# Second cross attention, selection: exponentials already normalised on ScalarE, one head of four selected on GpSimd

## The chip, the cores and the metric

The kernel runs on one core of a Trainium2 chip. The metric is the device time of one launch in microseconds; less is better. Engines are named as in the profile: PE is TensorE, DVE is VectorE, ACT is ScalarE, POOL is GpSimd and SP is SyncE.

## The reference

The program is two layers of a small perceiver (cross attention, self attention, feed forward, twice) on `x` of 4 batches x 256 rows x 256. The change is in the cross attention of the second layer, which has 4 heads and reads a context of 4096 rows of 192 per batch:

```python
scores = einsum('bthd,bghd->bhtg', Q, K) / sqrt(32)        # 4096 per row and head
scores = where(vision_mask, scores, -inf)
topv, topi = top_k(scores, 32)
probs = softmax(topv)
attn = zeros_like(scores).at[..., topi].set(probs)
attn_mean = attn.mean(axis=1)                               # over the 4 heads
c_t = einsum('btg,bgd->btd', attn_mean, context @ Wv)
```

So each row keeps its 32 largest scores per head, weights them by a softmax over these 32, and the four heads are averaged.

## The kernel before

The stage is `stage_x1a`. A step p (0 to 15) is a batch, one of its two blocks of 128 rows, and two heads h; four steps make a batch, and two steps (p even, then p odd) make one block's mean over four heads. The score tile `SC[p % 2]` is 128 x 2 x 4096 in float32 and there are two of it; the first lies in S0, so the trace calls the two S and SC. Three tiles `PM` hold exponentials, two tiles `ACC` the means. Every engine runs the same loop over iterations n = 0 to 19, in its own fixed order:

- TensorE in iteration n: `flag(n-2)`; for n >= 4 the transposes (`turn(m, g)`, eight per mean tile m, four in an even n and four in the following odd n) and the products with the context (`product(m, g)`, eight matmul records each); the scores of step n in eight chunks of 512 columns (`scores(n, ch)`), into two PSUM slots. In odd iterations the four products come ahead of the scores, in even ones between them. In n % 4 = 3 and n % 4 = 0 it also projects the next batch's keys (`keys`, four chunks each).
- ScalarE: copies transposes (`turned`), score chunks (`copy(n, ch)`) and key chunks out of PSUM, copies a product's sum (`done`), and computes `weigh(n-1, h)`, an exponential of 128 x 4096 in one instruction, after chunks 3 and 6 (L1661). `copy(n, 0)` waits until VectorE has selected step n-2, since they share a score tile.
- VectorE: for step n-1 and each head, 32 MAX8 over 128 columns each (`candidates`, L1731) and then `top`, a chain of small instructions that finds the 32nd largest value T8 and whether the shortcut was valid (L1736 to L1750); for step n-2, `check` (a flag from TensorE, a branch that is normally skipped) and two `select`s (L1776: exponential times (score >= T8), 4096 wide, with the row sum as a second output). The selects stand after 32 of head 0's candidates in even n, after 16 in odd n.
- GpSimd for every selected head: the reciprocal of the sum by a power (L1847), a scaling by it and by 1/4 (L1852 or L1855), and an addition into `ACC` (L1857). The last step is added by VectorE (`add`, L1794).
- SyncE loads the context tiles `CN` for the products; each load waits for an earlier product.

`turn(m, 0)` and `turn(m, 4)` wait for the finished sum of step 2m+1. In n % 4 = 1 VectorE also normalises the next query (XN, L1717), in n % 4 = 3 it makes a mask row (MR, L1724). In this text e(p, h) is the exponential of step p and head h.

The order of ScalarE around the change is written out by hand:

```python
if ch in (3, 6) and 0 <= n - 1 < NP:
    weigh(n - 1, ch // 6)
```

Of the kernel before, what the change touches and what calls it, by code (L numbers as in the profile page):

```python
# [123 lines left out]
def build(nc, dr, spec, out):  # L124
    ctx = ExitStack()
    with ctx:
# [1347 lines left out]
        def stage_x1a(c, x1a, S0, t_x1c):  # L1474
# [6 lines left out]
            ACC = [sbt(c, f"ACC{i}", [128, NK]) for i in range(2)]  # L1481
            CN = [sbt(c, f"CN{i}", [128, 4, 192]) for i in range(2)]
# [12 lines left out]
            ON1, NG1 = sbt(c, "ON1", [128, 1]), sbt(c, "NG1", [128, 1])  # L1495
# [7 lines left out]
            FLAG, NMAX, SUM, REC = range(4)  # L1503
# [3 lines left out]
            QV, MRV, GI = sig("x1_query"), sig("x1_mask_row"), sig("x1_pool_set")  # L1507
# [32 lines left out]
            def by_vector(p, h):  # L1540

                return p == NP - 1

            def summed(p, k):
                return V.at(("sum", p, 1, k)) if by_vector(p, 1) else G.at(("sum", p, 1))
# [99 lines left out]
            def scalar(e):  # L1645
# [41 lines left out]
                for n in range(NP + 4):  # L1687
                    nb_ = query(n)
                    m, gs = context(n)
                    if nb_ is not None:  # L1690
                        q_turned(nb_)
                    for g in gs[0:2 if n % 2 == 0 else 4]:
                        turned(m, g)
                    if nb_ is not None:
                        q_copy(nb_)
                    if m is not None and gs[3] == 7:
                        done(m)
                    for ch in range(8):
                        if n % 4 == 0 and rekeyed(n, ch):
                            keys["scalar"](e, bank, *rekeyed(n, ch))  # L1700
                        if n < NP:
                            copy(n, ch)
                        if n % 4 == 3 and rekeyed(n, ch):
                            keys["scalar"](e, bank, *rekeyed(n, ch))
                        if m is not None and n % 2 == 0 and ch in (3, 5):
                            turned(m, gs[2 + (ch - 3) // 2])
                        if ch in (3, 6) and 0 <= n - 1 < NP:
                            weigh(n - 1, ch // 6)

            def vector(e):  # L1710
# [41 lines left out]
                def check(p):  # L1752
# [6 lines left out]
                    e.wait_ge(*S.at(("e", p, 1)))  # L1759
# [3 lines left out]
                    with e.If_ne(reg["v"], 2 * 128 * 8):  # L1763
                        for h in range(2):
                            for r8 in range(4):
                                e.max(t8[:, h, 8 * r8:8 * r8 + 8], sc[:, h, :])
                                e.drain()
                                e.match_replace(sc[:, h, :], t8[:, h, 8 * r8:8 * r8 + 8], sc[:, h, :], SENT)
                                e.drain()
                            e.tensor_scalar(sc[:, h, :], sc[:, h, :], 0.9 * SENT, None, ALU.is_le)  # L1770
                            e.memset(t8[:, h, 31:32], 0.5)
                            e.drain()

                def select(p, h):
                    pm = PM[(2 * p + h) % 3]
                    e.scalar_tensor_tensor(pm[:, :], SC[p % 2][:, h, :], T8[p % 2][:, h, 31:32], pm[:, :], ALU.is_ge, ALU.mult,  # L1776
                                           accum_out=SM[p % 3][:, h, SUM:SUM + 1]).then_inc(*V.up(("sel", p, h)))

                def add():

                    p = NP - 1
                    sm, acc = SM[p % 3], ACC[1]
                    for h in range(2):
                        rc = sm[:, h, REC:REC + 1]
                        e.wait_ge(*V.at(("sel", p, h)))
                        e.tensor_scalar(rc, sm[:, h, SUM:SUM + 1], 4.0, None, ALU.mult).then_inc(*V.up())
                        e.wait_ge(*V.now())
                        e.reciprocal(rc, rc).then_inc(*V.up())
                    e.wait_ge(*G.at(("sum", p - 1, 1)))
                    for k in range(2):  # L1790
                        part = slice(k * NK // 2, (k + 1) * NK // 2)
                        for h in range(2):
                            e.wait_ge(*V.now())
                            e.scalar_tensor_tensor(acc[:, part], PM[(2 * p + h) % 3][:, part], sm[:, h, REC:REC + 1], acc[:, part], ALU.mult, ALU.add).then_inc(*V.up(("sum", p, h, k)))  # L1794
# [18 lines left out]
                for n in range(NP + 4):  # L1813
# [4 lines left out]
                    for h in range(2):  # L1818
                        for g in range(32):
# [12 lines left out]
            def gpsimd(e):  # L1832
                e.memset(NG1[:, :], -1.0).then_inc(*GI.up())
# [3 lines left out]
                for p in range(NP):  # L1837
                    b, k, hp = place(p)
                    for h in range(2):
                        if by_vector(p, h):  # L1840
                            continue
                        pm, sm, acc = PM[(2 * p + h) % 3][:, :], SM[p % 3], ACC[k]
                        rc = sm[:, h, REC:REC + 1]
                        e.wait_ge(*V.at(("sel", p, h)))
                        if p + h == 0:
                            e.wait_ge(*GI.now())
                        e.tensor_tensor(rc, sm[:, h, SUM:SUM + 1], NG1[:, :], ALU.pow).then_inc(*G.up())  # L1847
                        if hp + h == 0:
                            if b > 0:
                                e.wait_ge(*M.at(("t", 2 * (b - 1) + k, 7)))  # L1850
                            e.wait_ge(*G.now())
                            e.tensor_scalar(acc[:, :], pm, rc, 0.25, ALU.mult, ALU.mult).then_inc(*G.up(("sum", p, h)))  # L1852
                        else:
                            e.wait_ge(*G.now())
                            e.tensor_scalar(pm, pm, rc, 0.25, ALU.mult, ALU.mult).then_inc(*G.up())  # L1855
                            e.wait_ge(*G.now())
                            e.tensor_tensor(acc[:, :], acc[:, :], pm, ALU.add).then_inc(*G.up(("sum", p, h)))  # L1857

            def sync(e):
# [12 lines left out]
                def context_in(m, g):  # L1872
# [5 lines left out]
                    elif g < 5:  # L1878
                        e.wait_ge(*V.at(("sel", NP - 2, 1)))
# [8 lines left out]
                for n in range(NP + 4):  # L1888
# [16 lines left out]
                    if n == NP + 1:  # L1905
                        e.wait_ge(*V.at(("sel", NP - 2, 1)))
# [959 lines left out]
```

## Time and profile before

| | us |
|---|---|
| median of 3 runs | 2086.05 |
| lowest, highest run | 2084.93, 2088.73 |
| time of the profiled execution | 2084.4 |
| its span | 2082.6 |
| first and last instruction of the selection, L1731 to L1794 | 1151.9 to 1700.5 |

The profiled execution's time is 1.8 us more than its span. A row of the timeline gives the start, the duration and the instruction; `x32` behind it means that so many were merged, and the bracket gives the idle time ahead of it and what ended it.

### The profile page before, as it was taken

The numbers are of one execution on the slowest core, as the hardware profiler recorded it, in microseconds if no ns is written. First come the engines' busy times: TensorE is split into PE (matmuls) and PEld (weight loads), VectorE is DVE, ScalarE is ACT, GpSimd is POOL, SyncE is SP. The second block draws the span as 40 slices with busy tenths as digits, with TensorE's granted clock in tenths as the row PEclk, the third lists the DMA queues.
The fourth block names the chain that finished last, engine by engine and source line by source line (L and its number), as shares of the span: only waits on it lengthen the run. The fifth ranks groups of instructions, "written<-read, shape, count | busy, mean of one in ns | idle before, by whom it ended". The sixth has DMA issues, their size and how long they took to land.

```text
span 2082.6 us, 34689 instructions
## 1 busy us (share of the span) xinstructions
PE 1755.0 (84%) x13676; PEld 1114.9 (54%) x13676; DVE 1214.4 (58%) x2969; ACT 1025.3 (49%) x1391; POOL 753.6 (36%) x660
## 2 busy tenths in 40 slices
PE   6889999999999998888788868777777658987884
PEld 3445655565565555565577325344553455776663
DVE  5154241415333202636784698999999967547776
ACT  2578578667766991211311545546565521114542
POOL 6364334414533400000300076978779721110001
PEclk9999999999999998999788557788886779999987
DMA  7865649655664712000100003122231251000000
GB/s 153 168 114 125 136 110 139 136 117 123 131 129 102 112 61 80 2 1 2 54 1 6 9 16 86 52 85 76 69 93 37 74 189 68 0 1 1 1 6 16
DMA packets 80061, 150.01 MB, mean 72 GB/s; under 512 B 15464, under 2 KB 65448, under 8 KB 73480
## 3 DMA queue, kind: packets, MB, share of 16 engines
q1 hardware_dynamic: 64304, 101.80, 17.1%
q0 software_dynamic: 12336, 41.41, 12.9%
q10 hardware_dynamic: 3240, 4.35, 0.8%
q8 instruction: 118, 1.93, 0.4%
q14 instruction: 63, 0.52, 0.1%
HBM read 93.59 MB, written 2.62 MB: 46 GB/s over the span
## 4 chain that ended last, share of the span: by engine, by line
PE 62%; DVE 23%; POOL 4%; ACT 4%; issue 3%; DMA 2%; ACTq 0%; DVEq 0%; POOLq 0%; SPq 0%
PE R L112 37%; PE B L112 22%; DVE CA L1731 5%; DVE PM L1776 5%; PE B L178 2%; POOL ACC L1857 2%; DVE CA L1743 1%; DVE T L1745 1%; ACT PS L2415 1%; ACT PM L1661 1%; DMA CN<-in_ctxn 1%; DMA KST<-OV 1%; DVE MX L2571 1%; POOL PM L1855 1%; DVE A L1067 1%
## 5 line engine op out<-in xcount | busy, mean ns | idle before, releaser
L629 ACT ACTIVATE P<-R 128x1024 f32<-128x1024 f32 x512 | 500.8, 1028 | 128.0 <-PE R L112 113.7
L112 PE MATMUL R<-QS,KST 100*128 100x256 bf16 x2048 | 270.7, 275 | 13.0 <-issue 7.4
L112 PE MATMUL B<-P,VP 128*32 128x256 f32 x4096 | 277.4, 387 | 1.4 <-issue 1.1
L112 PEld LDWEIGHTS R<-QS,KST 100*128 100x128 bf16 x2048 | 182.0, 98 | 138.5 <-issue 64.6
L1857 POOL TENSOR_TENSOR ACC<-ACC,PM 128x4096 f32<-128x4096 f32 x22 | 195.1, 8869 | 1.8
L200 POOL TENSOR_TENSOR LNrs<-LNve,pk_const 128x2 f32<-128x2 f32 x36 | 25.3, 703 | 445.6 <-DVE LNve L196 445.3
L112 PE MATMUL R<-OV,QT 32*128 32x512 f32 x512 | 179.2, 786 | 0.0
L837 POOL DMA_DIRECT2D KST<-OV x300 | 144.5, 490 | 66.5 <-PE R L112 46.4
L112 PEld LDWEIGHTS B<-P,VP 128*32 128x32 f32 x4096 | 107.7, 109 | 102.5 <-issue 33.8
L1847 POOL TENSOR_TENSOR SM<-SM,NG 128x1 f32<-128x1 f32 x30 | 79.3, 2643 | 144.2 <-DVE PM L1776 144.2
L659 DVE CAST OV<-RT 128x512 bf16<-128x512 f32 x64 | 31.4, 490 | 168.4 <-ACT RT L116 99.7
L791 POOL CAST OV<-RT 128x512 bf16<-128x512 f32 x64 | 39.0, 610 | 207.1 <-DVE RT L661 207.1
L1731 DVE MAX8 CA<-S 128x8 f32<-128x128 f32 x512 | 101.8, 275 | 12.0 <-ACT S L116 11.6
L672 DVE COPY VP<-R 128x512 f32<-128x512 f32 x54 | 34.8, 686 | 126.8 <-PE R L112 126.8
L1731 DVE MAX8 CA<-SC 128x8 f32<-128x128 f32 x512 | 100.9, 276 | 6.6 <-ACT SC L116 6.0
L756 DVE RECIPROCAL RC<-B 128x256 f32<-128x256 f32 x16 | 28.0, 1751 | 119.1 <-PE B L112 119.1
L116 ACT ACTIVATE S<-R 128x1024 f32<-128x1024 f32 x64 | 64.1, 1024 | 61.4 <-DVE PM L1776 34.8
L112 PE MATMUL R<-CT,pk_x 128*128 128x512 f32 (+1 forms) x224 | 87.0, 636 | 6.8 <-ACT RT L116 6.8
L112 PE MATMUL R<-OV,ONB 1*128 1x512 bf16 x256 | 61.9, 480 | 35.9 <-ACT SC L116 22.0
L112 PEld LDWEIGHTS R<-OV,QT 32*128 32x128 f32 x512 | 64.0, 246 | 37.0 <-issue 29.5
L116 ACT ACTIVATE SC<-R 128x1024 f32<-128x1024 f32 x64 | 64.1, 1020 | 37.2 <-PE R L112 20.9
L1855 POOL TENSOR_SCALAR PM<-PM,SM 128x4096 f32<-128x4096 f32 x22 | 80.9, 3679 | 2.2
(346 smaller groups left out, 3374.1 us busy)
## 6 DMA issues: line engine op xcount, KB each, us to landing
KST<-OV POOLq DMA_DIRECT2D x276, 128.0 KB, 10.7
CT<-in_ctxP SPq DMA_DIRECT2D x40, 768.0 KB, 4.8
CN<-in_ctxn SPq DMA_DIRECT2D x60, 384.0 KB, 3.4
CT<-in_ctxT SPq DMA_DIRECT2D x64, 192.0 KB, 2.5
KST<-OV SPq DMA_DIRECT2D x84, 128.0 KB, 8.9
KST<-in_ctxP ACTq DMA_DIRECT2D x4, 768.0 KB, 8.0
pk_a<-in_pk_a SPq DMA_DIRECT2D x1, 3014.0 KB, 9.7
OV<-in_pk_x1b SPq DMA_DIRECT2D x1, 2944.5 KB, 9.9
```

Source lines behind the costliest of these rows:

```text
L112: return e.matmul(o, l, r, start=st, stop=sp, skip_group_check=True)
L116: return e.activation(o, i, ACT.Copy)
L178: return e.transpose(o, i, ident[0:n, 0:n])
L629: e.activation(P[(32 * p + k0) % 3][:, :], ring.at(("s", p, k0))[:, :], ACT.Exp).then_inc(*EX.up((p, k0)))
L672: e.tensor_copy(o, v).then_inc(*VC.up((b, 4 * ch + h + 2 * i)))
L791: e.tensor_copy(KS[1][:, cs], rt[:, :]).then_inc(*KG.up())
L837: e.dma_start(KST[buf][16 * s:16 * s + 16, hh, cols], KS[SLOT_K[s]][r0:r0 + 16, cols]).then_inc(*S[buf].up((b, g) if hh == hs[-1] and s == ...
L1731: e.max(CA[:, g * 8:g * 8 + 8], SC[p % 2][:, h, g * 128:g * 128 + 128]).then_inc(*V.up())
L1776: e.scalar_tensor_tensor(pm[:, :], SC[p % 2][:, h, :], T8[p % 2][:, h, 31:32], pm[:, :], ALU.is_ge, ALU.mult, accum_out=SM[p % 3][:, h, SU ...
L1847: e.tensor_tensor(rc, sm[:, h, SUM:SUM + 1], NG1[:, :], ALU.pow).then_inc(*G.up())
L1855: e.tensor_scalar(pm, pm, rc, 0.25, ALU.mult, ALU.mult).then_inc(*G.up())
L1857: e.tensor_tensor(acc[:, :], acc[:, :], pm, ALU.add).then_inc(*G.up(("sum", p, h)))
```

## The change

- `weigh(p, h)` on ScalarE becomes four activations: an exponential of the 32 kept values with their sum as a second output, `Ln` of four times that sum, `Identity` that makes the bias (minus maximum, minus logarithm), and the exponential of 128 x 4096 with this bias, which then comes out divided by four times the row sum. It waits for the end of `top` (`fl`) where it waited for its third instruction (`nm`).
- `weigh(n-1, 0)` stands after chunk 5 (before: 3), and `weigh(n-1, 1)` at the very start of iteration n+1, ahead of everything else of ScalarE (before: after chunk 6 of n).
- The weights of p even, h = 0 are written straight into `ACC`; the scaling and the power of GpSimd, and the sums of `select`, are gone.
- For p even, h = 1, VectorE no longer selects. GpSimd makes a mask in bfloat16 (`MK`, score >= T8), multiplies the exponential by it, and adds. `copy(n, 0)` then waits for that mask (n even) and for the exponentials of step n-2.
- The selects stand after 16 candidates of head 0 in every n. `check` no longer waits for the exponential; each `select` does.
- The branch that is normally skipped has a longer body. `add` becomes four plain additions. The scratch area of the descriptors of GpSimd's DMAs is set to 4096 bytes.

The diff, cut to its core (the rest follows from these lines):

```diff
+            MK = sbt(c, "MK", [128, NK], BF16)
+            TE = sbt(c, "TE", [128, 32])
+            def weights(p, h):
+                return (ACC[p // 2 % 2] if p % 2 + h == 0 else PM[2 * (p % 2) + h - 1])[:, :]
+            def by_gpsimd(p, h):
+                return p % 2 == 0 and h == 1
...
                 def weigh(p, h):
-                    i = 2 * p + h
-                    if i >= 3:
-                        e.wait_ge(*G.at(("sum", *divmod(i - 3, 2))))
-                    e.wait_ge(*V.at(("nm", p, h)))
-                    e.activation(PM[i % 3][:, :], SC[p % 2][:, h, :], ACT.Exp, bias=SM[p % 3][:, h, NMAX:NMAX + 1], scale=RS).then_inc(*S.up(("e", p, h)))
+                    sm = SM[p % 3][:, h, :]
+                    e.wait_ge(*V.at(("fl", p, h)))
+                    e.activation(TE[:, :], T8[p % 2][:, h, 0:32], ACT.Exp, bias=sm[:, NMAX:NMAX + 1], scale=RS, accum_out=sm[:, LSUM:LSUM + 1]).then_inc(*S.up())
+                    e.wait_ge(*S.now())
+                    e.activation(sm[:, LSUM:LSUM + 1], sm[:, LSUM:LSUM + 1], ACT.Ln, scale=4.0).then_inc(*S.up())
+                    e.wait_ge(*S.now())
+                    e.activation(sm[:, BIAS:BIAS + 1], sm[:, LSUM:LSUM + 1], ACT.Identity, bias=sm[:, NMAX:NMAX + 1], scale=-1.0).then_inc(*S.up())
+                    if p % 2 + h == 0 and p >= 4:
+                        e.wait_ge(*M.at(("t", (p - 4) // 2, 7)))
+                    if p % 2 + h > 0 and p >= 2:
+                        e.wait_ge(*G.at(("sum", p - 2, h)))
+                    e.wait_ge(*S.now())
+                    e.activation(weights(p, h), SC[p % 2][:, h, :], ACT.Exp, bias=sm[:, BIAS:BIAS + 1], scale=RS).then_inc(*S.up(("e", p, h)))
                 def copy(p, ch):
                     if ch == 0 and p >= 2:
-                        e.wait_ge(*V.at(("sel", p - 2, 1)))
+                        e.wait_ge(*(G.at(("mask", p - 2)) if by_gpsimd(p - 2, 1) else V.at(("sel", p - 2, 1))))
+                        e.wait_ge(*S.at(("e", p - 2, 1)))
...
+                    if 0 <= n - 2 < NP:
+                        weigh(n - 2, 1)
                     if nb_ is not None:
                         q_turned(nb_)
...
-                        if ch in (3, 6) and 0 <= n - 1 < NP:
-                            weigh(n - 1, ch // 6)
+                        if ch == 5 and 0 <= n - 1 < NP:
+                            weigh(n - 1, 0)
...
                 def select(p, h):
-                    pm = PM[(2 * p + h) % 3]
-                    e.scalar_tensor_tensor(pm[:, :], SC[p % 2][:, h, :], T8[p % 2][:, h, 31:32], pm[:, :], ALU.is_ge, ALU.mult,
-                                           accum_out=SM[p % 3][:, h, SUM:SUM + 1]).then_inc(*V.up(("sel", p, h)))
+                    e.wait_ge(*S.at(("e", p, h)))
+                    e.scalar_tensor_tensor(weights(p, h), SC[p % 2][:, h, :], T8[p % 2][:, h, 31:32], weights(p, h), ALU.is_ge, ALU.mult).then_inc(*V.up(("sel", p, h)))
...
-                            if h == 0 and g == (31 if n % 2 == 0 else 15) and 0 <= n - 2 < NP:
+                            if h == 0 and g == 15 and 0 <= n - 2 < NP:
                                 check(n - 2)
                                 select(n - 2, 0)
-                                select(n - 2, 1)
+                                if not by_gpsimd(n - 2, 1):
+                                    select(n - 2, 1)
...
+                for p in range(NP - 1):
+                    acc = weights(p - p % 2, 0)
                     for h in range(2):
+                        pm = weights(p, h)
+                        if p % 2 + h == 0:
                             continue
+                        e.wait_ge(*V.at(("sel", p, 0 if by_gpsimd(p, h) else h)))
+                        if by_gpsimd(p, h):
                             e.wait_ge(*G.now())
+                            e.tensor_scalar(MK[:, :], SC[p % 2][:, h, :], T8[p % 2][:, h, 31:32], None, ALU.is_ge).then_inc(*G.up(("mask", p)))
+                            e.wait_ge(*S.at(("e", p, h)))
                             e.wait_ge(*G.now())
+                            e.tensor_tensor(pm, pm, MK[:, :], ALU.mult).then_inc(*G.up(("product", p)))
+                        e.wait_ge(*G.now())
+                        e.tensor_tensor(acc, acc, pm, ALU.add).then_inc(*G.up(("sum", p, h)))
...
-    nc = _bacc.Bacc("TRN2", target_bir_lowering=False, num_devices=1)
+    nc = _bacc.Bacc("TRN2", target_bir_lowering=False, num_devices=1, dynamic_dma_scratch_size=4096)
```

## Rows read from the trace of the kernel before

**Rows 1.** Windows, sum of iterations n=6 to 9: us, then busy us.

```profile
sum 131.10, PE 99.10 PEld 62.59 DVE 125.35 ACT 75.46 POOL 103.37; mean PE 24.77 PEld 15.65 DVE 31.34 ACT 18.86 POOL 25.84
```

**Rows 2.** The chain that ended last, stretch 1322 to 1454.

```profile
by line: DVE CA L1731 37.8%; DVE PM L1776 28.1%; DVE CA L1743 8.5%; DVE T L1745 8.3%; DVE CA L1748 3.4%; issue 3.0%; DVE XN L1717 2.2%; DVE T L1737 2.1%; DVE MR L1724 1.9%; DVE SM L1750 1.6%; DVE SM L1736 1.3%; DVEq L1762 0.9%; DVE SM L1739
```

**Rows 3.** Groups of instructions, 1167 to 1721: busy us, mean ns, idle before.

```profile
L1857 POOL TENSOR_TENSOR ACC<-ACC,PM 128x4096 f32<-128x4096 f32 x22 | 195.1, 8869 | 1.8
...
L1731 DVE MAX8 CA<-SC 128x8 f32<-128x128 f32 x512 | 100.9, 276 | 6.6 <-ACT SC L116 6.0
...
L1855 POOL TENSOR_SCALAR PM<-PM,SM 128x4096 f32<-128x4096 f32 x22 | 80.9, 3679 | 2.2
...
L1776 DVE SCALAR_TENSOR_TENSOR PM<-SC,T,PM 128x4096 f32<-128x4096 f32 x16 | 72.1, 4541 | 9.2 <-ACT PM L1661 3.8 <-DVE FI L1757 3.6 <-ACT S L116 1.8
...
L116 ACT ACTIVATE SC<-R 128x1024 f32<-128x1024 f32 x64 | 64.1, 1020 | 37.2 <-PE R L112 20.9 <-DVE PM L1776 14.3 <-DVE CA L1731 1.7
L1661 ACT ACTIVATE PM<-SC,SM 128x4096 f32<-128x4096 f32 x16 | 59.3, 3707 | 9.7 <-DVE SM L1739 9.7
```

**Rows 4.** Timeline, GpSimd and VectorE, n=6: start us, us, instruction.

```profile
1322.10 8.83 POOL L1857 TENSOR_TENSOR ACC<-ACC,PM 128x4096 f32<-128x4096 f32 x1
...
1329.84 5.38 DVE L1776 SCALAR_TENSOR_TENSOR PM<-S,T,PM 128x4096 f32<-128x4096 f32 x1 [0.59 <-DVE FI L1757]
...
1335.15 4.47 DVE L1776 SCALAR_TENSOR_TENSOR PM<-S,T,PM 128x4096 f32<-128x4096 f32 x1
1335.31 4.73 POOL L1847 TENSOR_TENSOR SM<-SM,NG 128x1 f32<-128x1 f32 x1 [4.37 <-DVE PM L1776]
```

**Rows 5.** Timeline, VectorE: one top(), and the start of iteration n = 9.

```profile
1350.42 0.21 DVE L1736 TENSOR_REDUCE SM<-CA 128x1 f32<-128x32 f32 x1
...
1354.53 0.27 DVE L1750 TENSOR_SCALAR SM<-SM,T 128x1 f32<-128x1 f32 x1
...
1420.34 2.89 DVE L1717 TENSOR_SCALAR XN<-X,MV,RSD 128x256 f32<-128x256 f32 x2
```

**Rows 6.** Timeline, ScalarE: small activations and table loads.

```profile
1769.23 1.28 ACT L2087 ACT_TABLE_LOAD   x1
...
1878.60 0.20 ACT L2435 ACTIVATE EDA<-pk_qf 128x1 f32<-128x1 f32 x1 [19.94 <-PEq L183]
...
1878.93 1.28 ACT L2438 ACT_TABLE_LOAD   x1
1880.22 0.20 ACT L2438 ACTIVATE EDA<-EDA 128x1 f32<-128x1 f32 x1
...
1888.16 0.19 ACT L2415 ACTIVATION_READ_ACCUMULATOR PS<-R,MX 128x1 f32 x1
```

**Rows 7.** Timeline, TensorE: iterations n = 7, 8 and 9 at the full clock.

```profile
1368.79 0.39 PE L112 MATMUL R<-OV,ONB 1*128 1x512 bf16 x2
...
1379.41 1.99 PE L112 MATMUL B<-CT,pk_x1a 96*128 96x256 f32 x8
...
1404.11 1.57 PE L112 MATMUL R<-CN,AT 128*128 128x192 f32 x8
...
1415.00 1.02 PE L112 MATMUL R<-OV,QT 32*128 32x512 f32 x4
...
1428.70 1.57 PE L112 MATMUL R<-CN,AT 128*128 128x192 f32 x8 [0.74 <-ACT AT L116]
...
1435.66 1.54 PE L112 MATMUL R<-CN,AT 128*128 128x192 f32 x8 [0.32 <-DMA CN<-in_ctxn]
```

**Rows 8.** Timeline, TensorE at iteration n = 10, after a wait for GpSimd.

```profile
1462.37 1.94 PE L178 MATMUL B<-pk_const,ACC 128*128 128x128 f32 x8 [7.82 <-POOL ACC L1857]
...
1468.62 2.93 PE L112 MATMUL R<-CN,AT 128*128 128x192 f32 x8
```

**Rows 9.** Windows, n=10 after that wait: busy us, granted clock, DMA.

```profile
1462.40:1472.40 10.00, 10.00 (x34) 6.35 (x36) 9.90 (x10) 2.63 (x4) 5.63 (x2) 0.50 0.01 2
```

More of the change, by code:

```diff
@@ L1494, in stage_x1a @@
             SM = [sbt(c, f"SM{i}", [128, 2, 4]) for i in range(3)]
[L1495 removed]
+            TE = sbt(c, "TE", [128, 32])
+            ON1 = sbt(c, "ON1", [128, 1])
             ONB = sbt(c, "ONB", [128, 128], BF16)
@@ L1538, in query @@
                 return n // 4 + 1 if n % 4 == 1 and n // 4 + 1 < NB else None
-            def by_vector(p, h):
-                return p == NP - 1
+            def weights(p, h):
+                return (ACC[p // 2 % 2] if p % 2 + h == 0 else PM[2 * (p % 2) + h - 1])[:, :]
+            def by_gpsimd(p, h):
+                return p % 2 == 0 and h == 1
             def summed(p, k):
-                return V.at(("sum", p, 1, k)) if by_vector(p, 1) else G.at(("sum", p, 1))
+                return V.at(("sum", p, 1, k)) if p == NP - 1 else G.at(("sum", p, 1))
             def tensor(e):
@@ L1772, in check @@
                             e.drain()
+                            total = t8[:, h, 33:34]
+                            e.scalar_tensor_tensor(weights(p, h), sc[:, h, :], 0.5, weights(p, h), ALU.is_ge, ALU.mult, accum_out=total)
+                            e.drain()
+                            e.tensor_scalar(total, total, 4.0, None, ALU.mult)
+                            e.drain()
+                            e.reciprocal(total, total)
+                            e.drain()
+                            e.tensor_scalar(weights(p, h), weights(p, h), total, None, ALU.mult)
+                            e.drain()
                 def select(p, h):
-                    pm = PM[(2 * p + h) % 3]
-                    e.scalar_tensor_tensor(pm[:, :], SC[p % 2][:, h, :], T8[p % 2][:, h, 31:32], pm[:, :], ALU.is_ge, ALU.mult,
-                                           accum_out=SM[p % 3][:, h, SUM:SUM + 1]).then_inc(*V.up(("sel", p, h)))
+                    e.wait_ge(*S.at(("e", p, h)))
+                    e.scalar_tensor_tensor(weights(p, h), SC[p % 2][:, h, :], T8[p % 2][:, h, 31:32], weights(p, h), ALU.is_ge, ALU.mult).then_inc(*V.up(("sel", p, h)))
                 def add():
                     p = NP - 1
[L1782 to L1788, printed above, removed]
+                    acc = weights(p - 1, 0)
+                    e.wait_ge(*V.now())
                     e.wait_ge(*G.at(("sum", p - 1, 1)))
@@ L1792, in add @@
                         for h in range(2):
+                            e.tensor_tensor(acc[:, part], acc[:, part], weights(p, h)[:, part], ALU.add).then_inc(*V.up(("sum", p, h, k)))
                             e.wait_ge(*V.now())
-                            e.scalar_tensor_tensor(acc[:, part], PM[(2 * p + h) % 3][:, part], sm[:, h, REC:REC + 1], acc[:, part], ALU.mult, ALU.add).then_inc(*V.up(("sum", p, h, k)))
                 def stats(n, a0, a1):
@@ L1878, in context_in @@
                     elif g < 5:
-                        e.wait_ge(*V.at(("sel", NP - 2, 1)))
+                        e.wait_ge(*G.at(("mask", NP - 2)))
                     else:
@@ L1905, in sync @@
                     if n == NP + 1:
-                        e.wait_ge(*V.at(("sel", NP - 2, 1)))
+                        e.wait_ge(*G.at(("mask", NP - 2)))
                         for g in (2, 3, 4):
```

24 lines of the change are left out of this document (3 added, 21 removed).

## The prediction

> **What bounds the kernel now.** I read three views of the stage. The windows first: four iterations (n = 6 to 9, two steps p even and two odd) take 131.1 us, and VectorE is busy for 125.35 of them, GpSimd for 103.4, TensorE for 99.1, ScalarE for 75.5 [rows 1]. Then the chain that ended last over the same stretch: nearly all of it is VectorE's candidates and selects [rows 2]. So a microsecond taken from VectorE there is worth one, until another engine's own order becomes longer. The groups give the prices [rows 3]: 32 MAX8 take 6.3 us (their starts are 0.197 apart, 100.9 us busy over 512), a select 4.48, an addition on GpSimd 8.87, a one-input pass there 3.68, a full exponential 3.70, a copied score chunk 1.02. One `top` takes 4.4 us (from 1350.42 to 1354.80 [rows 5]).
>
> Third, the timeline shows what two engines do to each other. A select that met a running addition took 5.38 us instead of 4.48, and ended its wait where the addition ended; GpSimd's power beside a select took 4.73 us, until the select was over [rows 4]; XN took 2.89 us [rows 5]. So an addition or product of GpSimd and a select of VectorE exclude each other, whichever starts first keeps the other out for its whole length.
>
> **The change, engine by engine.** VectorE loses one select in four: 2 x 4.48 = 9.0 us per four iterations, some 0.5 us of read sums (6 selects without one) and the 0.9 us of that blocked select. If nothing else ended later, four iterations would take 131.1 - 10.4 = 120.7 us. The last additions stay at four halves of select's length. The 16 checks and their skipped branch stay, with a longer body that I take at nothing.
>
> GpSimd loses powers and scalings and gains a mask and a product. Per two steps, before: 103.4 / 2 = 51.7 us. After: three additions and a product at 8.87 and a mask at 3.68 (a one-input pass of that width; the bounds are 3.68 and 8.87, and I take the one-input row), 39.2 us [rows 1, 3]. It is not the bound.
>
> ScalarE gains in each of 32 `weigh`s: an exponential of 32 columns with its sum (0.20 for a tiny activation, and 0.19 to read the sum; I take 0.40), Ln 0.20, Identity with its bias from memory 0.30 (bounds 0.20 and twice that), and table loads. A load takes 1.28 us, and the activation behind it starts at once, 0.01 us later [rows 6]. The trace shows no Ln. The bounds are no load (all functions in one table) and two (to Ln's table and back). The nearest row is Tanh followed by Exp, two functions with a load between them, so I take two: 2.58 us. The sum is 3.48, a `weigh` takes 3.48 + 3.70 = 7.15 us net of the usual overlap. That is 8 x 3.45 = 28 us more ScalarE per four iterations, 103 of 131 busy. By busy time it fits. By order it does not, since ScalarE waits for TensorE inside the same iteration.
>
> The Trainium skill, "ScalarE: Activation LUTs", section "What ACT_TABLE_LOAD costs", puts a switch at 2.66 us with its drain; the rows show 1.28 and nothing behind it. By the page eight `weigh`s would cost 22 us more than in my sum; by the rows they don't.
>
> **Four iterations stepped through.** TensorE's runs between two things that ScalarE must do come from [rows 7]: from the first product of an even n to score chunk 5, keys in between, 11.9 us (1404.11 to 1416.02), 8.1 without the two key projections of 1.9; the four products of an odd n 8.5 us (1428.70 to 1437.20); six score chunks and three key projections 12.6 us (1368.79 to 1381.40), 6.6 without keys. During the old order ScalarE did an exponential amid these runs, so TensorE could get ahead; in the new one only chunks 6 and 7 are left behind each `weigh`. I start with n = 8 at 0, ScalarE 8.0 us late, and step on until the lateness repeats.
>
> n = 8: e(6,0) ends at 5.4, select(6,0) at 9.9, the mask at 13.6. Then half the candidates, `top`, the other head: VectorE reaches n = 9 at 28.1. ScalarE: e(6,1) at 15.15; transposes, keys and copies with TensorE to 29.2; e(7,0) at 36.4; the rest to 39.0. GpSimd multiplies from 15.15 and adds until 32.9.
>
> n = 9: e(7,1) ends at 46.1. XN waits for GpSimd until 32.9, and the flag for score chunk 7, which needs the key chunk that ScalarE copied at 37.0; so select(7,0) ends at 45.2. GpSimd has been waiting for it and starts its addition, 8.9 us. select(7,1) could start at 46.1, and starts at 54.1. It ends at 58.6, and VectorE reaches n = 10 at 76.8. Before, the second select followed the first at once and the addition came after. ScalarE: products, copies from 58.6, e(8,0) at 73.3, free at 75.3.
>
> n = 10: e(8,1) at 84.0, mask at 89.0, copies from there, e(9,0) at 105.0, free at 107.0. VectorE reaches n = 11 at 103.5, GpSimd's addition ends at 106.8.
>
> n = 11: MR waits for that addition, select(9,0) ends at 115.5. e(9,1) ends at 114.2, 1.3 us ahead of that, so select(9,1) follows at once, to 119.9; VectorE reaches n = 12 at 138.2. ScalarE: products to 123.3, scores and keys to 136, e(10,0) at 143.6, free at 146.2, again 8.0 late.
>
> So four iterations take 138.2 instead of 131.1 us, +7.1. The work of steps 1 to 15 has fourteen iterations, 3.5 times that: **+25 us**. What follows VectorE's last iteration (the last transposes, context loads and products) hangs on the last flag and additions, which keep their distance from it, and is as long as before. The profiled execution took 2084.4 us and should come to 2109; the median of the runs, 1.7 us above it, to 2111.
>
> **The rivals.** (a) *No table loads in the loop*, chance 0.12. Exp, Ln and Identity stay in one table. For it: Tanh at 1878.60 ran on the table loaded for Gelu at 1769.23. Against it: the load between Tanh and Exp [rows 6]. `weigh` then takes 4.6 us, ScalarE is back at VectorE's boundaries, select(7,1) is ready before select(7,0) ends, and VectorE's 120.7 us bound the loop: -10.4 x 3.5 = -36, 2050 us. The Trainium skill, "ScalarE: Activation LUTs", section "Table sets: the hidden batching unit", says that Exp and Ln share one set and cost one load; by that rule this rival would be the result.
>
> (b) *The loads fit*, two per `weigh` but VectorE still bounding, chance 0.08. It needs ScalarE some 3 us earlier per iteration, since otherwise e(7,1) misses the end of select(7,0). Then part of (a): -10, 2076.
>
> (c) *No change that can be told*, chance 0.10. A change under 0.2% (4.2 us) can't be told from none here. If e(7,1) came 1 us earlier, the addition would not get ahead of select(7,1), and the loop would be the longer of ScalarE's own: 8 x 7.15 and 74.5 of the runs, copies and transposes = 131.7, +2, 2088.
>
> (d) *The forecast*, chance 0.50, its own range 2096 to 2122.
>
> (e) *TensorE drops to its lower level*, chance 0.18. After 7.8 us of waiting in n = 10 its granted clock was 0.50 over ten us, the lower level, 1.2 GHz [rows 9], and eight product records took 2.93 us [rows 8] instead of 1.57 at 2.4 GHz [rows 7]. In the new order it stands still around each `weigh`, 5 us and more. If the first product, transposes and scores of each iteration run at that level, ScalarE slips by 3 to 4 us in each, and e(9,1) misses select(9,0) too, since its margin is 1.3 us. That is another 7 us per four iterations: +50, 2136, at worst 2150.
>
> (f) *The smaller scratch area stalls GpSimd's DMAs* in the first layer, chance 0.02. Its bursts there are short, and I give it +10.
>
> **How the numbers follow.** Slower are (d), (e), (f): 0.70. Same is (c): 0.10. Faster are (a) and (b): 0.20. The predicted time is that of (d), 2111. The range takes in (e) but for its worst, and goes down to (b) and part of what lies between it and (a): 2070 to 2142; left out are (a), 0.12, and some 0.06 above.
>
> **What would show it.** Two rows ACT_TABLE_LOAD per `weigh`, 64 in all, at 1.28. In n = 9 and its like, a select that starts some 8 us after the first ended, with "POOL" holding it back; in n = 11 none. VectorE's busy time in the stage down by some 35 us, and its idle time up by more. ScalarE busy about 100 of 138 us. Four iterations of 138 us. A prediction of slower is wrong if the loads are few, or if `weigh` takes under 6 us.

## The result, and the profile after

The changed kernel takes 2162.47 us (median of 4, 2150.79 to 2165.89) against 2087.39 for the kernel before (median of 4): the ratio is 1.0342, 95% interval 1.0291 to 1.0394. It is slower, as forecast, but by 75 us and not by 25. The profiled execution took 2165.89 us, its span is 2164.1. The page's first part:

```profile
PE 1804.4 (83%) x13676; PEld 1145.5 (53%) x13676; DVE 1207.6 (56%) x2925; ACT 1136.2 (53%) x1583; POOL 726.5 (34%) x615
```

I measure the selection from its first MAX8 over 128 columns to its last one. Before, that is one window (us, then busy us of PE, PEld, DVE, ACT, POOL, then TensorE's granted clock, DMA share, GB/s):

```profile
1151.90:1674.90 523.00, 389.39 (x1660) 226.20 (x1656) 481.02 (x1571) 284.21 (x247) 377.32 (x82) 0.73 0.22 65
```

The same window after, and three times four iterations within it:

```profile
1158.40:1751.10 592.70, 433.35 (x1660) 255.65 (x1656) 469.18 (x1533) 388.27 (x433) 342.02 (x37) 0.67 0.18 53
...
1221.30:1375.60 154.30, 115.11 (x398) 65.47 (x395) 124.95 (x391) 99.41 (x110) 94.48 (x11) 0.61 0.16 47
1375.60:1527.70 152.10, 111.47 (x474) 69.93 (x474) 124.83 (x391) 102.54 (x116) 94.54 (x11) 0.74 0.22 63
1527.70:1680.50 152.80, 117.84 (x466) 73.66 (x465) 117.29 (x387) 101.65 (x114) 94.44 (x11) 0.71 0.22 63
```

So 69.7 of the 81.5 us between the two spans lie in the selection; 6.5 lie ahead of it and 5.3 behind. Four iterations take 153.1 us (forecast 138.2, before 131.1 [rows 1]), and in them VectorE is busy for 122.4. It no longer bounds them. TensorE does the same instructions in 44 us more of busy time, at a granted clock of 0.67 and not 0.73. The groups that answer to [rows 3] and [rows 6] (busy us, mean ns, idle before):

```profile
L1871 POOL TENSOR_TENSOR ACC<-ACC,PM 128x4096 f32<-128x4096 f32 x22 | 207.3, 9423 | 90.9 <-DVE PM L1802 89.9
...
L1802 DVE SCALAR_TENSOR_TENSOR PM<-SC,T,PM 128x4096 f32<-128x4096 f32 x16 | 98.1, 6153 | 30.3 <-ACT PM L1675 26.0 <-DVE FI L1774 2.7 <-ACT SM L1669 0.9
L1866 POOL TENSOR_SCALAR MK<-S,T 128x4096 bf16<-128x4096 f32 x8 | 84.9, 10611 | 162.3 <-DVE ACC L1802 162.3
...
L1869 POOL TENSOR_TENSOR PM<-PM,MK 128x4096 f32<-128x4096 f32 x8 | 63.7, 7961 | 1.2
...
L1667 ACT ACT_TABLE_LOAD x32 | 41.1, 1283 | 0.6
L1675 ACT ACT_TABLE_LOAD x32 | 41.1, 1283 | 2.1
```

The mask costs 10.61 us, three times the forecast's 3.68. The 64 table loads take 1.28 us as priced, and the product 7.96 where 8.87 was taken. One iteration shows how it goes wrong. Timeline of the changed kernel around n = 11 (starts at 1528.2); first TensorE, still at the end of n = 10, then ScalarE, VectorE and GpSimd:

```profile
1539.08 1.92 PE L112 MATMUL R<-OV,QT 32*128 32x512 f32 x4
1540.92 2.93 PE L112 MATMUL R<-CN,AT 128*128 128x192 f32 x8
1543.78 0.24 PE L112 MATMUL B<-ON,SM 128*1 128x1 f32 x4
...
1552.12 2.93 PE L112 MATMUL R<-CN,AT 128*128 128x192 f32 x8 [6.79 <-ACT AT L116]
...
1544.67 1.28 ACT L1667 ACT_TABLE_LOAD   x1
...
1546.57 1.28 ACT L1675 ACT_TABLE_LOAD   x1
1547.87 3.71 ACT L1675 ACTIVATE PM<-SC,SM 128x4096 f32<-128x4096 f32 x1
...
1528.21 3.17 DVE L1748 MAX8 CA<-S 128x8 f32<-128x128 f32 x16
1544.06 0.14 DVE L1774 CAST FI<-B 1x1 int32<-1x1 f32 x1 [12.68 <-PE B L112]
1544.80 4.49 DVE L1802 SCALAR_TENSOR_TENSOR PM<-SC,T,PM 128x4096 f32<-128x4096 f32 x1 [0.59 <-ACT TE L1665]
1551.61 10.88 DVE L1802 SCALAR_TENSOR_TENSOR PM<-SC,T,PM 128x4096 f32<-128x4096 f32 x1 [2.33 <-ACT PM L1675]
...
1549.36 8.84 POOL L1871 TENSOR_TENSOR ACC<-ACC,PM 128x4096 f32<-128x4096 f32 x1 [12.25 <-DVE PM L1802]
```

Read it from the left. TensorE is late with its last products and score chunks, and slow: four matmuls of a chunk take 1.92 us and a product 2.93, where [rows 7] have 1.02 and 1.57, so it is at the lower of its two levels, 1.2 GHz [rows 8, 9]. The flag of step 9 stands behind them in its queue, and VectorE waits 12.68 us for it. The first select is then over at 1549.3, GpSimd starts its addition, the second exponential ends at 1551.6, and select(9, 1) ends at 1562.5 where 1556.1 was due. TensorE meanwhile waits 6.79 us for a transposed tile that ScalarE copies only after that exponential.

The window of TensorE ahead of that flag has it busy without a gap, at a granted clock of 0.50:

```profile
1525.59:1543.78 18.19, 18.19 (x54) 11.10 (x53) 5.65 (x24) 12.37 (x14) 11.44 (x2) 0.50 0.15 43
```

Its three products and four chunk halves take some 8 us more than at the prices of [rows 7] (3 x 1.36 + 4 x 0.9, an estimate). So in this iteration some 8 of the 12.68 us of waiting come from the lower level, unless ScalarE had held TensorE up instead. Some waits of the selection as sums (us, times, longest):

```profile
ACT S L116 <- POOL MK L1866: 37.1, 7, 6.3
DVE FI L1774 <- PE B L112: 32.8, 6, 12.7
PE R L112 <- ACT AT L116: 26.8, 7, 8.9
DVE PM L1802 <- ACT PM L1675: 26.0, 7, 4.6
DVE FI L1774 <- PE R L112: 24.2, 5, 13.4
```

### The profile page after: what moved, and what is told of

It reads as the page before. It is cut to its first block and busy times, and to the rows that moved or that the text cites. A ratio compares the mean times of both kernels' runs of the same rounds, so it can differ in the third digit from the quotient of the medians.

```text
span 2164.1 us, 34798 instructions
## 1 busy us (share of the span) xinstructions
PE 1804.4 (83%) x13676; PEld 1145.5 (53%) x13676; DVE 1207.6 (56%) x2925; ACT 1136.2 (53%) x1583; POOL 726.5 (34%) x615
## 5 line engine op out<-in xcount | busy, mean ns | idle before, releaser
L1871 POOL TENSOR_TENSOR ACC<-ACC,PM 128x4096 f32<-128x4096 f32 x22 | 207.3, 9423 | 90.9 <-DVE PM L1802 89.9
L112 PE MATMUL R<-OV,QT 32*128 32x512 f32 x512 | 197.3, 860 | 0.0
L1866 POOL TENSOR_SCALAR MK<-S,T 128x4096 bf16<-128x4096 f32 x8 | 84.9, 10611 | 162.3 <-DVE ACC L1802 162.3
L112 PE MATMUL R<-OV,ONB 1*128 1x512 bf16 x256 | 66.5, 515 | 66.1 <-ACT S L116 25.3
L1802 DVE SCALAR_TENSOR_TENSOR PM<-SC,T,PM 128x4096 f32<-128x4096 f32 x16 | 98.1, 6153 | 30.3 <-ACT PM L1675 26.0
L112 PE MATMUL R<-CN,AT 128*128 128x192 f32 x288 | 78.0, 432 | 38.6 <-ACT AT L116 27.3
L112 PEld LDWEIGHTS R<-CN,AT 128*128 128x128 f32 x288 | 66.0, 258 | 58.5 <-ACT AT L116 32.8
## 6 DMA issues: line engine op xcount, KB each, us to landing
KST<-OV POOLq DMA_DIRECT2D x276, 128.0 KB, 10.6
OV<-in_pk_x1b SPq DMA_DIRECT2D x1, 2944.5 KB, 10.5
```

The source lines that it names most:

```text
L112: return e.matmul(o, l, r, start=st, stop=sp, skip_group_check=True)
L1802: e.scalar_tensor_tensor(weights(p, h), SC[p % 2][:, h, :], T8[p % 2][:, h, 31:32], weights(p, h), ALU.is_ge, ALU.mult).then_inc(*V.up(("s ...
L1866: e.tensor_scalar(MK[:, :], SC[p % 2][:, h, :], T8[p % 2][:, h, 31:32], None, ALU.is_ge).then_inc(*G.up(("mask", p)))
L1871: e.tensor_tensor(acc, acc, pm, ALU.add).then_inc(*G.up(("sum", p, h)))
```

## The experiments

The whole kernel repeats within about 10 us either way, and much of that can lie ahead of the selection: it begins at 1151.9 us in the profile before and at 1166.2 in that of e2. So besides the ratio each table gives the length of the selection in one profile. It repeats closely in the kernel before (523.0 us, 523.1 in e2), less so in the changed one: e1 and e16, which have the same selection with instructions added behind it, take 589.3 and 596.8 us, against 592.7. Differences under some 8 us between two selections are not told from this spread.

In e5, e6, e12 and e17 two multiplications stand in the mask's place: one head of four is scaled and not selected. These four show where the time goes, and leave a part of the work out.

**What GpSimd charges (e1, e16).** The changed kernel with one-off instructions of GpSimd behind its work, each on 128 x 4096:

```diff
+                steps = [lambda: e.tensor_scalar(MK[:, :], sc, t8, None, ALU.is_ge),
+                         lambda: e.tensor_scalar(MK[:, :], sc, t8, None, ALU.mult),
+                         lambda: e.tensor_scalar(MK[:, :], sc, 0.5, None, ALU.is_ge),
+                         lambda: e.tensor_scalar(MK[:, :], sc, t8, 0.25, ALU.is_ge, ALU.mult),
+                         lambda: e.tensor_scalar(MK[:, :], sc, t8, 0.25, ALU.mult, ALU.mult),
...
```

> The changed kernel with eleven one-off GpSimd instructions of 128 x 4096 behind the last addition of the stage, for their prices alone; the span gets longer by their sum and says nothing. Two theories of why the mask took 10.61 us where 3.68 was forecast. Theory A, the comparison: is_ge is slow whatever it writes, so is_ge into float32 takes 10.6 and a multiplication into bfloat16 3.7. Theory B, the output type: writing bfloat16 is slow, so the multiplication and the copy into bfloat16 take about 10 and is_ge into float32 3.7. The product with a bfloat16 operand took 7.96 in the changed kernel against 8.87 for two float32 operands, and should do so here.

In that order (the line numbers are the list's), then the comparison into float32:

```profile
1772.01 10.61 POOL L1875 TENSOR_SCALAR MK<-SC,T 128x4096 bf16<-128x4096 f32 x1 [18.08 <-DVE ACC L1813]
1782.71 10.62 POOL L1876 TENSOR_SCALAR MK<-SC,T 128x4096 bf16<-128x4096 f32 x1
1793.42 10.54 POOL L1877 TENSOR_SCALAR MK<-SC 128x4096 bf16<-128x4096 f32 x1
1804.05 14.05 POOL L1878 TENSOR_SCALAR MK<-SC,T 128x4096 bf16<-128x4096 f32 x1
1818.20 3.69 POOL L1879 TENSOR_SCALAR MK<-SC,T 128x4096 bf16<-128x4096 f32 x1
1821.98 10.61 POOL L1880 TENSOR_SCALAR PM<-SC,T 128x4096 f32<-128x4096 f32 x1
```

Neither reason I had holds. A lone multiplication costs as much as a lone comparison, and the output's type nothing. What is short is the pair of two multiplications, which is the row that I had priced the mask by [rows 3]. e16 tried other pairs.

> The changed kernel with six more one-off GpSimd instructions at its end, each 128 x 4096 but the last: multiplication of two tensors, one a broadcast column; multiply and add; add and multiply; subtract and multiply; maximum and multiply; one comparison over 512 columns. If only multiplications have the short way, multiply and add takes 10 us or more; if every pair without a comparison has it, all pairs take 3.7 us (the comparison with a multiplication took 14.05). The broadcast product 7.9 to 8.9 us if it goes as any tensor by tensor. The comparison over 512 columns 1.3 us if the price is in the elements (10.61 / 8), more if part of it is fixed.

A product with a broadcast column, multiply and add, add and multiply, subtract and multiply, maximum and multiply, and one comparison over 512 columns:

```profile
1787.00 7.01 POOL L1876 TENSOR_TENSOR PM<-SC,T 128x4096 f32<-128x4096 f32 x1 [18.07 <-DVE ACC L1813]
1794.11 3.68 POOL L1877 TENSOR_SCALAR MK<-SC,T 128x4096 bf16<-128x4096 f32 x1
1797.88 3.68 POOL L1878 TENSOR_SCALAR MK<-SC,T 128x4096 bf16<-128x4096 f32 x1
1801.66 14.07 POOL L1879 TENSOR_SCALAR MK<-SC,T 128x4096 bf16<-128x4096 f32 x1
1815.82 14.04 POOL L1880 TENSOR_SCALAR MK<-SC,T 128x4096 bf16<-128x4096 f32 x1
1829.96 1.57 POOL L1881 TENSOR_SCALAR MK<-SC,T 128x512 bf16<-128x512 f32 x1
```

Neither expectation fits: pairs of multiply and add in either order have the short way too, a subtraction or a maximum in the pair has not. Neither a constant threshold (10.54 in e1) nor shorter pieces (eight of 1.57 are 12.6 us) would have made the mask cheap.

**The scratch area (e2).** The kernel before, with the one argument added.

> The kernel before with only the scratch area of GpSimd's DMAs cut to 4096 bytes. The stretch ahead of the selection took 6.5 us longer in the profile of the changed kernel than in that of the kernel before (1158.4 against 1151.9). If the scratch area causes that, this kernel takes 2093 us and its selection starts near 1158. If it is the spread of single executions, it takes 2087 plus or minus 3.

2077.09 us (10 runs) against 2086.21, ratio 0.9968 (0.994 to 0.9997); selection 523.1 us. It costs nothing: rival (f) is out.

**Three terms, each taken back alone and together (e3, e5, e6, e10, e11, e12, e17).** One table, loaded ahead of the stage; a short instruction in the mask's place; the exponentials at their old places:

```diff
+                e.preload_act_table_set("natural_log_exp_and_others")
```
```diff
-    e.tensor_scalar(MK[:, :], SC[p % 2][:, h, :], T8[p % 2][:, h, 31:32], None, ALU.is_ge)
+    e.tensor_scalar(MK[:, :], SC[p % 2][:, h, :], T8[p % 2][:, h, 31:32], 0.25, ALU.mult, ALU.mult)
```
```diff
-                    if 0 <= n - 2 < NP:
-                        weigh(n - 2, 1)
...
-                        if ch == 5 and 0 <= n - 1 < NP:
-                            weigh(n - 1, 0)
+                        if ch in (3, 6) and 0 <= n - 1 < NP:
+                            weigh(n - 1, ch // 6)
```

> The changed kernel with the table that holds both Exp and Ln loaded once, ahead of the stage: no load is left in the loop and weigh takes 4.7 us instead of 7.24. Theory 1, ScalarE's longer weigh is the cause: nearly all of the loss goes, 2085 to 2100 us. Theory 2, the mask of 10.6 us is the main cause, because it holds back the copies of every even iteration: less than half of the 75 us come back, 2125 to 2150.

> The changed kernel with the mask's comparison replaced by two multiplications into the same tile, which e1_forms timed at 3.69 us instead of 10.61; one head of four is then not selected but scaled, so the output is not the reference's. All else, the 64 table loads too, is as in the changed kernel. Theory M, the mis-sized mask is what the forecast missed: this kernel behaves as forecast, 2100 to 2120, some 45 us below the changed one. Theory S, the steps through ScalarE and TensorE were too optimistic by themselves: it stays above 2135.

> Both: the mask at 3.69 us as in e5_short_mask (one head not selected, so not the reference's output) and no table load in the loop, as in e3_one_table. If these two terms are all that stood between the change and its gain, VectorE bounds the loop and the time falls to rival (a)'s, 2050 to 2070. If something else holds (the additions that exclude selects, TensorE's lower level), it stays at 2080 or above.

> The changed kernel (selection 592.7 us, ratio 1.034) with weigh(n-1, 0) and weigh(n-1, 1) after chunks 3 and 6 of iteration n again; table loads, GpSimd's mask and the selects after 16 candidates stay. Theory O: the loads hurt mostly because seven microseconds of weigh stand ahead of the transposes that TensorE waits for; selection under 570 us, ratio under 1.025. Rival P: 585 to 600 us, ratio 1.030 to 1.040.

> As e3 (one table, ratio 1.0216, selection 559.9 us), with the exponentials at their old places. Theory O: under 545 us, ratio under 1.012. Rival P: 555 to 565 us, ratio 1.018 to 1.025, since the mask of 10.61 us still holds back the first copy of each even iteration.

> As e6 (one table, two multiplications of 3.69 us where the mask stood, so that one head of four is scaled and not selected; ratio 1.0061, selection 521.9 us), with the exponentials at their old places. Theory O: with mask, loads and places all taken back, VectorE's saved select shows at last; selection 490 to 508 us, ratio 0.985 to 0.994. Rival P: TensorE's and ScalarE's own work is the longer chain whatever the places; 515 to 525 us, ratio 1.000 to 1.008.

> The changed kernel with two multiplications of 3.69 us for the mask (one head of four scaled, not selected) and the exponentials at their old places; the 64 table loads stay. If the loads add to the other terms, the selection is some 497 + 54 = 551 us, ratio 1.015 to 1.022. If the long mask had been hiding part of them, as at the new places (32.8 us with it, 52.9 without), it is 565 us or more, ratio over 1.022. If under 535 us, the loads hurt only together with the mask.

| table loads | mask | places | run | selection, us | ratio (95%) |
|---|---|---|---|---|---|
| 64 | 10.61 | new | the change | 592.7 (589.3 and 596.8 in e1 and e16) | 1.0342 (1.0291 to 1.0394) |
| 64 | 3.69 | new | e5 | 574.9 | 1.0262 (1.0211 to 1.0314) |
| 64 | 10.61 | old | e10 | 586.7 | 1.0386 (1.0334 to 1.0438) |
| 64 | 3.69 | old | e17 | 564.8 | 1.0236 (1.019 to 1.0282) |
| none | 10.61 | new | e3 | 559.9 | 1.0216 (1.0171 to 1.0262) |
| none | 3.69 | new | e6 | 521.9 | 1.0061 (1.0031 to 1.009) |
| none | 10.61 | old | e11 | 533.0 | 1.0089 (1.0064 to 1.0114) |
| none | 3.69 | old | e12 | 501.1 | 0.992 (0.9891 to 0.995) |

The differences within the table: the loads cost 33 to 64 us, most where nothing else holds the loop up; the mask's length 18 to 38 us; the new places 21 to 27 us without loads, and 6 to 10 us with them, where neither ratio nor selection tells them from nothing. With all three taken back the selection is 21.9 us shorter than before. The window of e12:

```profile
1163.40:1664.60 501.20, 414.34 (x1655) 241.07 (x1652) 442.58 (x1534) 310.06 (x370) 310.59 (x38) 0.71 0.22 67
```

e3 (2127.15 us) came out as the theory had it in which the mask is the main cause, and e5 (2137.35 us) went against that theory: by the selections the mask's length explains 18 of 70 us, by the ratios 0.8 of 3.4%, with intervals that overlap.

How the mask's length costs differs with the places. In e3 the selects of n = 3, 7, 11 and 15 took 11.2 to 12.5 us, each beside an addition of GpSimd; in e6 all took 4.5. VectorE's busy time in the selection falls from 479.8 us in e3 to 442.4 in e6, which is the 38 us by which the selection gets shorter.

e6, at 2094.19 us and 521.9, showed a third term, since 2050 to 2070 was due. Its iteration n = 9, on TensorE, then on VectorE:

```profile
1401.28 3.75 PE L112 MATMUL R<-CT,pk_x1a 96*128 96x256 f32 x8 [6.55 <-DMA CT<-in_ctxT]
...
1417.99 1.57 PE L112 MATMUL R<-CN,AT 128*128 128x192 f32 x8
...
1432.01 2.93 PE L112 MATMUL R<-CN,AT 128*128 128x192 f32 x8
...
1435.15 0.15 DVE L1775 CAST FI<-R 1x1 int32<-1x1 f32 x1 [11.47 <-PE R L112]
```

The flag comes late again. TensorE had stood still for 6.55 us, here for a context tile and not for ScalarE, and was at its lower level from 1401.3 to 1415.7 and once more after a wait of 2.4 us; between these it ran at the upper one (a product in 1.57 us). e11 and e12 bore the places out as expected; e10, with the loads kept, did not. In e17 the loads cost 63.7 us where I expected 54 (from 497 us for e12, whose selection is 501.1). With the long mask they cost 53.7 at the old places and 32.8 at the new ones, against 53.0 with the short one. That it hides a part of them shows clearly at the new places alone.

**One addition held back (e4).** GpSimd's first addition of an odd step waits for both selects.

```diff
-                        e.wait_ge(*V.at(("sel", p, 0 if by_gpsimd(p, h) else h)))
+                        e.wait_ge(*V.at(("sel", p, 0 if by_gpsimd(p, h) else 1)))
```

> The changed kernel with GpSimd's first addition of an odd step held back until both selects of the step are done. The trace after shows this addition ahead of the second select in the iterations n = 3, 7, 11 and 15, and the select 4.2 to 6.4 us longer. If that exclusion is a cause, four selects get back to 4.48 us and some 10 to 25 us come back, 2138 to 2152. If what VectorE gains there is waited for elsewhere, by ScalarE, the time stays within 5 us of 2162.

2150.79 us, ratio 1.0313 (1.0257 to 1.0369), selection 583.0. In n = 3, 7, 11 and 15 no select is blocked any more (4.49 us each, 18.9 less in all), and the selection is 9.7 us shorter than in the profile after, 6.3 and 13.8 than in e1 and e16; in the whole kernel the intervals overlap. This blocking is what the prediction had made the main cost.

**GpSimd's share taken away (e7, e8, e9).** `by_gpsimd` returns False, so VectorE does all selects; e8 has one table as well, and e9 also the old places, of selects too.

> One part of the change alone: ScalarE normalises (64 table loads), but VectorE selects all four heads again and GpSimd only adds, so there is no mask, no product, and the copies wait for a select again. Theory M: without the mask the copies of even iterations start earlier, but VectorE has 9 us more per four iterations and the additions meet more selects: 2110 to 2135. If the mask were a minor cause the time would be that of the changed kernel or more, 2160 and up.

> As e7_vector_selects, with the table of Exp and Ln loaded once. VectorE has the kernel before's work but for the read sums, with no wait for GpSimd's scaling, and no load: 2060 to 2080, faster than the kernel before by 10 to 20 us if the table loads are what spoils the normalising on ScalarE. If the longer and later weigh costs time even without loads, 2086 or more.

> The run before it with VectorE's selects and one table (e8) was 1.0074 of the kernel before, and its selection, from the first to the last MAX8 of 128 columns, lasted 526.5 us against 523.0. This kernel differs from it in places alone: weigh(n-1, 0) and weigh(n-1, 1) stand after chunks 3 and 6 again, and the selects after 32 candidates in even n. Theory O (the new places cost): selection 518 to 523 us, ratio 0.995 to 1.000. Rival P (the places don't matter; what is left is the longer weigh itself and the wait for the end of top): selection 526 us or more, ratio 1.005 or more.

Selections of 599.8, 526.5 and 533.6 us, ratios 1.0372 (1.0322 to 1.0422), 1.0074 (1.0045 to 1.0102) and 1.0092 (1.0065 to 1.0119). Without GpSimd's mask the loads cost 73 us. e7 had been expected at 2110 to 2135 us if the mask is the main cause and at 2160 or more if a minor one: it took 2159.94. So with the loads in place, giving VectorE all selects back and taking mask and product away changed nothing that can be told. e8 was to gain 10 to 20 us if the loads alone spoiled the change; at 2096.99 us it gained nothing. The old places gain nothing either when VectorE does all selects: that expectation of e9 failed, and why its selection is 10 us longer than before was not found.

**The same work with the mask moved (e13, e14, e15).** From e11: the mask starts when `top(p, 1)` ends (e13), is made in two halves with the copies waiting for the half they overwrite (e14), or both (e15).

```diff
-                        e.wait_ge(*V.at(("sel", p, 0 if by_gpsimd(p, h) else h)))
+                        e.wait_ge(*V.at(("fl", p, 1) if by_gpsimd(p, h) else ("sel", p, h)))
...
+                            for k in range(2):
+                                part = slice(k * NK // 2, (k + 1) * NK // 2)
+                                e.tensor_scalar(MK[:, part], SC[p % 2][:, h, part], T8[p % 2][:, h, 31:32], None, ALU.is_ge).then_inc(*G.up(("mask", p) if k else ("mask0", p)))
+                            e.wait_ge(*V.at(("sel", p, 0)))
```

> As e11 (one table, old places, selection 533.0 us, ratio 1.0089), but GpSimd starts the mask when top(p, 1) ends, where it waited for VectorE's 16 candidates, check and select(p, 0), some 8.6 us; its product waits for that select. Theory W (the mask costs because the first copy of the even iteration waits for its end): the mask ends 10.6 us after top, earlier than the short mask of e12 did (8.6 + 3.7); selection 490 to 508 us, ratio 0.988 to 0.996. Rival X (mask and select exclude each other as additions and selects do): select(p, 0) starts some 6 us later in every even iteration, selection 525 to 545 us, ratio 1.004 to 1.014.

> As e11, but the mask is made in two halves of 2048 columns, 5.3 us each, and the first copy waits for the first half alone, the fifth for the second. Theory W: copies start 5.3 of the 6.9 us earlier that separate e11 from e12; selection 503 to 518 us, ratio 0.994 to 1.002. Rival (GpSimd's length itself is what delays, through product and addition): 528 to 536 us, ratio 1.006 to 1.011.

> Early start and halves together. Theory W: no less than e13's gain and little more, since copies then hardly wait; selection 488 to 506 us, ratio 0.987 to 0.996. Rival X: as e13 there, 515 to 545 us.

| run | selection, us | median, us | ratio (95%) |
|---|---|---|---|
| e13 | 518.3 | 2072.48 | 0.9937 (0.9914 to 0.996) |
| e14 | 517.6 | 2080.02 | 0.9975 (0.9951 to 0.9999) |
| e15 | 499.1 | 2060.54 | 0.9893 (0.9865 to 0.9921) |

So at the old places it is not the mask's length that costs but when the score tile comes free. The waits of ScalarE's copies for the mask in e11 are 66.6 us; e12 has 16.8, and e15 none (6.1 for the select in its place).

```profile
ACT S L116 <- POOL MK L1865: 66.6, 7, 12.1
```

e13 fell between its two expectations, since the mask does hold a select up. In e13, VectorE's select ahead of GpSimd's mask; in e15, the select beside the two halves:

```profile
1454.89 6.92 DVE L1804 SCALAR_TENSOR_TENSOR ACC<-S,T,ACC 128x4096 f32<-128x4096 f32 x1 [0.61 <-DVE FI L1774]
...
1448.66 10.61 POOL L1868 TENSOR_SCALAR MK<-S,T 128x4096 bf16<-128x4096 f32 x1 [0.63 <-DVE SM L1767]
```
```profile
1454.28 4.52 DVE L1806 SCALAR_TENSOR_TENSOR ACC<-S,T,ACC 128x4096 f32<-128x4096 f32 x1 [0.61 <-DVE FI L1776]
...
1448.93 15.09 POOL L1872 TENSOR_SCALAR MK<-S,T 128x2048 bf16<-128x2048 f32 x2 [0.65 <-DVE SM L1769]
```

The select that met the whole mask ended 2.5 us behind it, as did six others of its eight. In e15 this one goes first between two halves, and the second half waits. So it is in the last four of the eight; the first four came after the second half had begun and took 5.3 to 7.4 us. **e15 is the version to keep:** it does all of the work, in 1.07% less time than the kernel before.

## Why the prediction was wrong

**What held.** Slower; two loads per `weigh`, 64 in all, at 1.28 us with the next activation at most 0.02 us behind, `weigh` at 7.24 us (1381.06 to 1388.30; forecast 7.15); VectorE's idle time up (42 to 124 us); the exclusion of an addition and a select; the tail (413 us behind the last candidates, 408 before). The Trainium skill, "ScalarE: Activation LUTs", section "What ACT_TABLE_LOAD costs", gives 2.66 us with a drain: this trace shows no drain. Its rule that Exp and Ln share one set (section "Table sets: the hidden batching unit") holds only in the kernels where that set is loaded ahead by hand; the changed kernel swaps twice in each `weigh`.

**The step that failed first: "I take the one-input row"** for the mask, 3.68 of the bounds 3.68 and 8.87. It measured 10.61, above both bounds, and 18 us of the selection hang on it (e5 against the change), 38 once the loads are gone. The row was two multiplications, and the price of GpSimd's `tensor_scalar` depends on its operations (e1). The 6.9 us more stand in front of ScalarE's first copy of each even iteration (37.1 us of waits in seven).

**The second: the four iterations stepped through, +7.1 us.** e5 has the mask at the price that I gave it. Its four iterations take 147.5 us (442.5 over twelve, from select(2, 0) to select(14, 0)) where 138.2 was due, and its selection is 51.9 us longer than before, not 25. The runs give the terms, taken one after the other from e12. The forecast's terms are rival (a)'s -36 and what leads from there to +25:

| term, us | forecast | measured | from |
|---|---|---|---|
| work taken from VectorE | -36 | -21.9 | e12 against before |
| new places, no loads | 0, in rival (a) | +20.8 | e6 against e12 |
| table loads | +61 | +53.0 | e5 against e6 |
| mask above 3.68 | 0 | +17.8 | the change against e5 |
| sum | +25 | +69.7 | |

In another order the terms come out otherwise, within the ranges given above. In this one the loads were not sized too low; the gain was too large by 14 us, and the move of the exponentials, which rival (a) put at nothing, costs 21 us by itself. The flag was wrong too: I had it down for a wait in n = 9 alone, and in e5 VectorE waits for flags 46.0 us in nine waits, the longest 13.1.

**How much TensorE's lower level has to do with it stays open.** That is rival (e), which I gave 0.18. Its 2136 us beside e5's 2137.35 is luck: by its ratio e5 stands at 2141 on the base of the prediction (2086.05), and it holds terms that (e) did not have. For (e): TensorE's busy time in the selection rose by 31 us in e5 and by 44 in the change, for the same instructions, and in n = 11 of the change some 8 of 12.68 us of a flag's lateness are the lower level, by the estimate above. Against it as the whole cause: with the loads taken out of e5 the clock stays and TensorE's busy time even grows, and yet the selection is 53 us shorter. The windows of e5, then e6:

```profile
1152.50:1727.40 574.90, 420.33 (x1660) 246.84 (x1656) 465.97 (x1533) 389.59 (x433) 293.58 (x38) 0.69 0.19 56
```
```profile
1161.70:1683.60 521.90, 430.21 (x1660) 251.20 (x1656) 442.40 (x1533) 311.97 (x370) 310.30 (x38) 0.69 0.21 64
```

The flags are as late in e6 as in e5 (48.5 us in nine waits). What went with the loads is 24 us of VectorE's busy time, which in e5 is mostly four selects of 8.6 to 11.3 us, and 29 us of its other waits. No run changed the clock alone.

**The blocked select** came in n = 11 and its like, not in n = 9: in n = 9 the flag held select(7, 0) back until both exponentials were there, and the two selects ran on end (8.88 us). In n = 11 e(9, 1) ended at 1551.6, 2.2 us behind the start of GpSimd's addition; the margin of 1.3 us was the right place to look. It is worth some 10 us in all (e4). Because blocked selects count as busy, VectorE's busy time fell by 12 us and not by 35.

**Rival (a)**, 2050 us without loads, would have been wrong too: e3 is 1.0216, and e6, which has (a)'s price for the mask as well, 1.0061. It took loads, mask and places together to see VectorE's gain (e12). Its four iterations take 127.8 us (383.4 over twelve), not 120.7, with flags still 28 us late in nine waits.

**The range** held (e) but for its worst, and left no room for a wrong price of the mask on top of a wrong stepping.

## What to carry to other kernels

Price an instruction by a row with the same operations, not by one with the same shape, and if there is none, keep an upper bound above the dearest row. Before a long activation is put ahead of copies that TensorE waits for, list what stands in TensorE's queue behind those copies, flags included, and price that stretch at both of its levels. A step that frees a shared buffer is worth moving early or cutting in half even when its engine has time to spare.

## What the hardware showed unexpectedly

- GpSimd's `tensor_scalar` on 128 x 4096: 3.68 to 3.69 us for multiply with multiply, multiply with add and add with multiply; 10.5 to 10.6 for a single comparison (into either type, with the threshold from memory or constant) or a single multiplication; 14.0 to 14.1 for a pair with a comparison, subtraction or maximum. A single comparison over 512 columns takes 1.57 us.
- GpSimd's one-input comparison holds up a select of VectorE, though not as long as an addition does. In e13 selects of 4.49 us took 5.1 to 9.1 beside the mask and seven of eight ended 2.5 us behind it; the eighth began 0.5 us ahead of the mask's end and took 4.49. The select that met an addition in n = 11 ended 4.3 us behind it (1562.5 against 1558.2). Why the mask lets the select go some 2 us earlier was not found.
- Stretches of TensorE that are equal in instructions differ by 44 us in busy time over the selection with the granted clock, 0.67 against 0.73.
